# Routing of the first sequence from x centered but not scaled, first weights loaded ahead, six loads issued by ScalarE

## The reference, cut to what matters

```
x = x + 0.5 * ffn(layernorm(x))
x = x + attn(layernorm(x))
x = x + 0.5 * ffn(layernorm(x))

def layernorm(x): m, v = mean(x), var(x); return (x - m) / sqrt(v + 1e-5)
def ffn(x):       # 64 experts, 128 -> 64 -> 128, top 8
    shared = silu(x @ Ws_up) @ Ws_down
    aff = x @ centroids.T
    idx = top_k(aff + expert_biases, 8)
    w = sigmoid(aff[idx]);  w = w / (sum(w) + 1e-8)
    cw = w scattered to a 512 x 64 table
    h = silu(x @ W_up[e]);  y = h @ W_down[e]
    return shared + sum over e of y * cw[:, e]
```

## Time and profile before

| | us |
|---|---|
| median of 3 runs | 812.16 (812.0 to 812.24) |
| profiled execution | 811.96 |
| its span, first to last instruction | 809.8 |
| busy PE / DVE / ACT / POOL | 800.3 / 649.3 / 619.9 / 424.5 |

### The profile page before, as it was taken

The page is one execution under the profiler, slowest core; times in us unless marked ns, Lnnn a source line. Parts: engine busy times, 40 slices in busy tenths (PEclk is TensorE's granted clock), DMA queues, the critical chain, the costliest instruction groups (busy, mean ns, idle before and its releaser), DMA issues.

```text
span 809.8 us, 12417 instructions
## 1 busy us (share of the span) xinstructions
PE 800.3 (99%) x3686; PEld 651.4 (80%) x3686; DVE 649.3 (80%) x1410; ACT 619.9 (77%) x1189; POOL 424.5 (52%) x378
## 2 busy tenths in 40 slices
PE   8999999999999999999999999999999999999998
PEld 5778878888888888888888888888888888888786
DVE  6987979779797787967879679796887778688865
ACT  5887777778777777868787678786787777786875
POOL 3885546555455554545545355463554545454453
PEclk9999999999999999999999999999999999999999
DMA  7000000000000000000000000000000000000000
GB/s 261 29 1 14 13 1 1 0 26 2 14 1 0 26 0 13 0 0 26 0 13 0 0 26 0 13 0 0 26 0 0 0 1 27 0 1 1 14 0 14
DMA packets 15901, 11.44 MB, mean 14 GB/s; under 512 B 1664, under 2 KB 14848, under 8 KB 15872
## 3 DMA queue, kind: packets, MB, share of 16 engines
q1 hardware_dynamic: 15872, 11.08, 4.4%
HBM read 8.98 MB, written 2.10 MB: 14 GB/s over the span
## 4 chain that ended last, share of the span: by engine, by line
PE 92%; DVE 3%; ACT 2%; POOL 2%; DMA 1%; SPq 0%; issue 0%; DVEq 0%
PE up L718 14%; PE up L719 14%; PE up L720 14%; PE y_ps L718 14%; PE y_ps L720 14%; PE y_ps L719 14%; PE side L727 3%; PE side L737 2%; PE side L759 1%; PE side L758 1%; POOL g_lo L357 1%; ACT g_hi L450 1%; DVE gated L596 1%; DVE up L596 1%; DVE g_lo L605 1%; DMA wu_raw<-in_w_up 1%
## 5 line engine op out<-in xcount | busy, mean ns | idle before, releaser
L357 POOL TENSOR_TENSOR g_lo<-gated,g_hi 128x512 fp32r<-128x512 f32 x256 | 333.9, 1305 | 343.6 <-ACT g_hi L450 342.9
L442 ACT ACTIVATE up<-up 128x512 f32<-128x512 f32 x528 | 309.6, 587 | 97.5 <-PE up L720 95.3
L596 DVE TENSOR_TENSOR gated<-up,cw 128x512 f32<-128x512 f32 x256 | 175.6, 686 | 83.4 <-ACT up L442 77.2
L718 PE MATMUL y_ps<-g_hi,wd_hi 128*128 128x512 f32 x512 | 207.8, 406 | 1.0 <-POOL g_lo L357 0.9
L720 PE MATMUL y_ps<-g_hi,wd_lo 128*128 128x512 f32 x512 | 202.6, 396 | 0.0
L718 PE MATMUL up<-x_hi,wu_hi 128*128 128x512 f32 x512 | 202.2, 395 | 0.3 <-POOL wu_lo L364 0.3
L719 PE MATMUL up<-x_lo,wu_hi 128*128 128x512 f32 x512 | 202.5, 396 | 0.0
L720 PE MATMUL up<-x_hi,wu_lo 128*128 128x512 f32 x512 | 201.7, 394 | 0.0
L719 PE MATMUL y_ps<-g_lo,wd_hi 128*128 128x512 f32 x512 | 201.5, 394 | 0.0
L450 ACT CAST g_hi<-up 128x512 fp32r<-128x512 f32 x272 | 160.6, 591 | 47.6 <-DVE up L596 44.5
L596 DVE TENSOR_TENSOR up<-up,cw 128x512 f32<-128x512 f32 x256 | 176.9, 691 | 21.0 <-ACT up L442 17.2
(11 more groups left out here) (101 smaller groups left out, 487.2 us busy)
## 6 DMA issues: line engine op xcount, KB each, us to landing
x_in<-in_x SPq DMA_DIRECT2D x8, 256.0 KB, 2.8
wu_raw<-in_w_up SPq DMA_DIRECT2D x4, 512.0 KB, 6.1
wd_raw<-in_w_down SPq DMA_DIRECT2D x4, 512.0 KB, 6.9
x_res<-in_x SPq DMA_DIRECT2D x8, 256.0 KB, 2.7
out<-out_sb SPq DMA_DIRECT2D x7, 256.0 KB, 2.2
out<-out_sb SPq DMA_DIRECT2D x2, 128.0 KB, 1.8
ident<-in_ident SPq DMA_DIRECT2D x1, 64.0 KB, 2.6
sm_raw<-in_ws_up SPq DMA_DIRECT2D x2, 32.0 KB, 2.3
```

The lines of the kernel that those rows point to most:

```text
L357: nc.gpsimd.tensor_tensor(g_lo[:, i, :], gated[:, t // 2 % ORING, :], g_hi[:, i, :].bitcast(fp32), ALU.subtract).then_inc(lo_done[1], 1)
L442: nc.scalar.activation(up[i][:, :], up[i][:, :], ACT.Silu).then_inc(silu_done, 1)
L596: nc.vector.tensor_tensor(gated[:, t // 2 % ORING, :] if t % 2 else up[i][:, :], up[i][:, :], cw[ph.q][:, :], ALU.mult).then_inc(gate_done, 1)
L718: nc.tensor.matmul(o, a[0], b[0], start=start, stop=False)
```

## The change

Only the start and phase 0 are touched.

- ScalarE issues six of the small loads, before everything else on its queue. SyncE, without them, issues the first four pieces of the weights directly after x and the identity; the second x comes behind the third pair of pieces.
- x for the routing is only centered (ScalarE, with the negated mean as bias), since the order of a row's affinities and their sum with the biases need the scale only afterwards. It is transposed into `up[2]` and `up[3]`, copied to `x_raw` by VectorE, half by half, and the affinities are multiplied by rstd as the bias is added; the Tanh of the sigmoid takes half of rstd as its scale.
- x for the products is made apart: ScalarE scales the centered x into `normed[1]`, TensorE transposes it into `up[4]`, ScalarE casts that to `x_hi`, VectorE subtracts for `x_lo`, now behind `take_top`.
- GpSimd makes `wu_hi` of the first two eighths of W_up itself; ScalarE did.
- The weights are spread in halves, transposed in halves (`side0`, `side1`) and copied in halves. `late` of phase 0 is 2 for TensorE and, as `late_act`, 1 for ScalarE; both were 3.
- Fill-in products: 8, 1 and none instead of 12, 3 and 3.

```
-WARM_START, WARM_ROWS, WARM_ROUTE = 12, 3, 3
+WARM_START, WARM_ROWS = 8, 1
-    "late": 3,
+    "late": 2, "late_act": 1,
...
             load_x(0, wait=False)
-            sp.dma_start(ce_raw[:, :], cent_t).then_inc(small_in[0], 16)
             sp.dma_start(ident[:, :], ident_in).then_inc(small_in[0], 16)
-            sp.dma_start(bias_b[:, :], ebias.partition_broadcast(P)).then_inc(small_in[0], 16)
-            for h in range(2):
-                sp.dma_start(sm_raw[:, SU + h * F:SU + (h + 1) * F], ws_up).then_inc(small_in[1], 16)
-                sp.dma_start(sm_raw[h * F:(h + 1) * F, SD:SD + D], ws_down).then_inc(small_in[1], 16)
             load_pieces(0)
             load_pieces(1)
-            load_x(1)
...
             load_pieces(2)
+            load_x(1)
...
-            split_up(0)
-            split_up(1)
+            for i in range(2):
+                js = slice(i * JS, (i + 1) * JS)
+                pool.wait_ge(wu_in[0], 16)
+                nc.gpsimd.tensor_copy(wu_hi[:, js, :], wu_raw[:, js, :]).then_inc(first_hi_done, 1)
+                split_up(i)
...
-                    cw_copy(ph.q, ph.use)
+                    if ph.first:
+                        act.wait_ge(first_cw_half, 1)
+                        nc.scalar.copy(cw[0][:, half(0, T)], side0[:, half(0, T)])
+                        act.wait_ge(cw_turned[0], 1)
+                        nc.scalar.copy(cw[0][:, half(1, T)], side1[:, half(1, T)]).then_inc(cw_done[0], 1)
...
+            nc.scalar.dma_start(ce_raw[:, :], cent_t).then_inc(route_in, 16)
+            nc.scalar.dma_start(bias_b[:, :], ebias.partition_broadcast(P)).then_inc(route_in, 16)
+            for h in range(2):
+                nc.scalar.dma_start(sm_raw[:, SU + h * F:SU + (h + 1) * F], ws_up).then_inc(small_in[1], 16)
+                nc.scalar.dma_start(sm_raw[h * F:(h + 1) * F, SD:SD + D], ws_down).then_inc(small_in[1], 16)
...
+            act.wait_ge(neg_mean_done, 1)
+            for m in range(NB):
+                made = nc.scalar.activation(normed[0][:, m, :], x_in[:, m, :], ACT.Identity, bias=neg_mean[:, m:m + 1])
...
+            for m in range(NB):
+                made = nc.scalar.activation(normed[1][:, m, :], normed[0][:, m, :], ACT.Copy, scale=rstd[0][:, m:m + 1])
+            made.then_inc(first_scaled, 1)
             act.wait_ge(x_turned[0], 1)
+            nc.scalar.copy(x_hi[0][:, :], up[RING - 1][:, :]).then_inc(x_hi_done[0], 1)
+            act.wait_ge(bias_done[0], 1)
+            act.wait_ge(half_rstd_done, 1)
+            for m in range(NB):
+                made = nc.scalar.activation(sig[:, m, :], aff[:, m, :], ACT.Tanh, scale=half_rstd[:, m:m + 1])
...
+            nc.vector.tensor_scalar_mul(neg_mean[:, :], mv[0][:, :, 0], -1.0).then_inc(neg_mean_done, 1)
...
+            for m in range(NB):
+                made = nc.vector.scalar_tensor_tensor(biased[:, m, :], aff[:, m, :], rstd[0][:, m:m + 1], bias_b[:, :],
+                                                      ALU.mult, ALU.add)
+            made.then_inc(bias_done[0], 1)
             find_top(0, 0)
             take_top(0, 0)
+            dve.wait_ge(x_hi_done[0], 1)
+            nc.vector.tensor_tensor(x_lo[0][:, :], up[RING - 1][:, :], x_hi[0][:, :].bitcast(fp32), ALU.subtract).then_inc(x_lo_done[0], 1)
             select(0, 0)
...
-                        if ph.first:
-                            keep_busy(WARM_ROUTE, side0, wu_hi[:, 0, :], wu_hi[:, 0:NB, :])
                         turn_cw(ph.q, ph.use, ph.first)
```

More of the change, by code:

```diff
@@ L464, in phase @@
                 if ph.late is not None:
-                    for t in range(ph.late + 1):
+                    for t in range(ph.late_act + 1):
                         silu(ph, t)
@@ L468, in phase @@
                             high_part(ph, 0)
-                    cw_copy(ph.q, ph.use)
+                    if ph.first:
[3 more added lines that the diff above has]
+                        nc.scalar.copy(cw[0][:, half(1, T)], side1[:, half(1, T)]).then_inc(cw_done[0], 1)
+                    else:
+                        cw_copy(ph.q, ph.use)
                     if not ph.first:
@@ L472, in phase @@
                 for t in range(SLOTS):
-                    if t < NT and (ph.late is None or t > ph.late):
+                    if t < NT and (ph.late is None or t > ph.late_act):
                         silu(ph, t)
@@ L698, in _ @@
             dve.wait_ge(inv_done[0], 1)
-            nc.vector.tensor_tensor(*spread_operands, ALU.mult).then_inc(first_dup_done, 1)
+            for h in range(2):
+                nc.vector.tensor_tensor(*(o[:, half(h, NB), :, :] for o in spread_operands), ALU.mult).then_inc(first_dup_done, 1)
             split_low(wd_lo, wd_raw, wd_hi, 0, wd_hi_done, wd_lo_done[0])
@@ L768, in up_product @@
                 w = (wu_hi[:, t - 1, :], wu_lo[:, t - 1, :]) if t > 0 else small(SU, SU + P)
-                split_product(o[:, :], w, (x_hi[q][:, :], x_lo[q][:, :]), True, True).then_inc(up_done, 1)
+                if ph.first and t == 0:
+                    nc.tensor.matmul(o[:, :], w[0], x_hi[q][:, :], start=True, stop=False)
+                    nc.tensor.matmul(o[:, :], w[1], x_hi[q][:, :], start=False, stop=False)
+                    pe.wait_ge(x_lo_done[q], 1)
+                    nc.tensor.matmul(o[:, :], w[0], x_lo[q][:, :], start=False, stop=True).then_inc(up_done, 1)
+                else:
+                    split_product(o[:, :], w, (x_hi[q][:, :], x_lo[q][:, :]), True, True).then_inc(up_done, 1)
             def down_product(ph, t):
@@ L810, in phase @@
                     if t == 0:
-                        pe.wait_ge(x_lo_done[ph.q], ph.use + 1)
+                        if ph.first:
+                            pe.wait_ge(x_hi_done[0], 1)
+                        else:
+                            pe.wait_ge(x_lo_done[ph.q], ph.use + 1)
                     if t < NT and before(t - RING)[1] < NT and not (ph.first and t < RING):
@@ L861, in _ @@
                 for m in range(h * NB // 2, (h + 1) * NB // 2):
-                    last = nc.tensor.transpose(rows((side0, side1)[h], m), normed[0][:, m, :], ident[:, :])
-                last.then_inc(half_turned if h == 0 else x_turned[0], 1)
+                    last = nc.tensor.transpose(rows(up[2 + h], m), normed[0][:, m, :], ident[:, :])
+                last.then_inc(half_turned, 1)
+            pe.wait_ge(route_in, 32)
+            pe.wait_ge(half_copied, 1)
+            affinity_blocks(0, range(0, NB // 2))
+            pe.wait_ge(x_copied[0], 1)
+            affinity_blocks(0, range(NB // 2, NB)).then_inc(aff_done[0], 1)
+            pe.wait_ge(first_scaled, 1)
+            turn(up[RING - 1], lambda m: normed[1][:, m, :]).then_inc(x_turned[0], 1)
             keep_busy(WARM_ROWS, y_ps[:, :], zeros_r[:, :], g_hi[:, 0, :])
-            affinities(0, 0)
             over_phases(pe, phase)
```

59 lines of the change are left out of this document (38 added, 21 removed).

## The result

The changed kernel takes **819.31 us** (median of 4 runs, 818.87 to 819.48) against 812.17: ratio 1.0087, interval 1.0071 to 1.0103. It is 7.1 us slower; 811.6 was forecast, within 809.9 to 813.3. The profiled execution took 819.14 us.

What follows compares the result with a forecast made beforehand. TensorE's own work was taken to bound the kernel, the start only shifting it through VectorE's gating of tile 5. A routing gain of 1.1 less 0.5 for a late Silu saves 0.6 us: 812.16 becomes 811.6, range 809.9 to 813.3.

Steps and rivals of the forecast that it cites:

- The bound: Whole kernel: TensorE busy 800.3 of 809.8 us, so a change to the start only shifts its steady stream.
- sm_hi after 6.22: ScalarE's start: the load for sm_hi is there in time, sm_hi done by 6.6, sigmoid 0.25 us before VectorE wants it.
- Rival (2): ScalarE's front is late, through waiting issues or small loads landing late among the pieces (814.0); chance 0.20.
- These edits cost nothing: Start: GpSimd's casts for the first two pieces and the later second x are hidden, low parts ready at 9.4 and 11.3.
- rival (1): More comes through: late Silu 3 free (0.5), normalisations' hold avoided (0.93), 2.0 us saved, 810.1; chance 0.22.
- the 5.06: ScalarE's start: six issues end at 3.55, then table load 1.28 and first Silu 0.21, so centring can begin.
- bias add: VectorE's routing: becomes four 128x64 operations, 0.75 us taken, 0.33 more than before, bounds 0.42 and 1.68.
- the late Silu: ScalarE, phase 0: Silu 3 falls between the casts of tiles 1 and 4, delaying gating of tile 5 by 0.50 us.
- the front: Routing up to VectorE's selection: selection at 10.8 against 12.04, 1.24 ahead, taken as 1.1 us after 0.15 for slow transposes.
- my case: Main forecast for the kernel: 0.6 us saved, 811.6, spreading over 811.0 to 812.4 by its bounds; chance 0.42.
- Rival (2)'s other form: Start: ScalarE's six issues take turns with SyncE's, 5.64 us instead of 2.82, ending at 814.4.
- Rival (3): TensorE stays at or falls back to its low clock with fewer fill-ins: 813.0, or 814.5 if it lasts; chance 0.16.

Runs made afterwards that it cites:

- e1: The changed kernel with all six small loads back on SyncE, ahead of the pieces: 813.98 us.
- e15: The changed kernel with all six small loads back on SyncE ahead of the pieces and the two new tensors declared last: 812.27 us.
- e8: The changed kernel, shared-expert loads on SyncE ahead of the pieces, new tensors last, late 3 for both engines, three fill-ins behind the transposes: 811.52 us.
- e2: The changed kernel, ScalarE still issuing the six loads, but SyncE waiting for the shared expert's four before issuing the first piece: 814.17 us.
- e3: The kernel before, with only the six small loads issued by ScalarE ahead of its table load: 817.49 us.
- e9: e8 with four unused tensors behind neg_half, 128 bytes: 797.57 us.
- e4: The kernel before, with the change's two new tensors declared and never used: 813.69 us.
- e5: The changed kernel with its two new tensors, neg_mean and half_rstd, declared last: 817.00 us.
- e7: The changed kernel with the old 12, 3 and 3 fill-in products again: 819.13 us.
- e17: The changed kernel with two more unused tensors behind its own two, 128 bytes in all: 802.92 us.

## Why the prediction was wrong

**The bound was read rightly.** The start moves TensorE's stream as a whole: the 1.51 us wait at 33.40 stands, unchanged in length, at 39.12, 34.53 (e1), 33.83 (e15) and 33.42 (e8).

**The step that failed: "sm_hi after 6.22 (its last load is issued at 3.1 and a load of this kind lands after 2.1 us, so it is there)".** It was issued at 3.46 and landed after 9.1. Rival (2) named this very case, but priced it with 5.8 us and so at 814.0, and gave it part of 0.20. The 5.8 was the landing of another load, of 64 KB, between pieces in one queue. The Trainium skill ("DMA: Bandwidth & Descriptors", Queues, rings and completion order) has each DMA engine alternate between the queues that have work, a packet from each. The trace agrees as far as it goes: between 3.5 and 10 us its packet record holds, in every 0.5 us, 30 to 47 packets of SyncE's queue (mostly 4096 bytes, 159 ns each by the median) and 22 to 46 of ScalarE's (mostly 256 bytes, 18 ns). The page's packet is of 9 to 17 descriptors, and the record doesn't say whether its own packets are such groups. At about one for one, small packets wait for large ones, and the six loads go at the pieces' pace. e1, e2 and e3 show the lateness and its cure; the alternation is read from the record and not from an edit. Delay through the chain: sm_hi 6.3 late against e15 (12.61 and 6.30), selection 6.4 (17.29 and 10.85), gating of tile 1 5.3 (20.75 and 15.46), for the late spread at least escapes the hold. In time it is 5.3 (e1 against the changed kernel). The low clock behind the wait has a part in it that no run separates: x's transposes before x_hi took 1.11 in place of 0.66.

**"These edits cost nothing" leaves out a hold.** GpSimd's work on the first two pieces is itself hidden, as said, and in the changed kernel, where GpSimd had ended at 17.65 before the spread began, the spread took 0.76; 0.79 was forecast. But once the loads are punctual, VectorE's selection and spread meet the low parts. The spread took 1.74 in e2 and e15, 0.95 over the forecast, and the selection 1.40 in e8. Before, wu_lo ended at 12.49 and the spread began at 13.48. Where the hold falls depends on when the pieces come, and e2 and e15 issue them later than the change does; but the forecast's own times, low parts ready at 9.4 and 11.3 and the selection at 10.8, put it on the selection, and it is in no term. I had used such a hold in rival (1) for the normalisation and not looked for it here. The rows are regular: wherever the selection begins while GpSimd is in a low part, it ends 0.27 to 0.29 us after that part (12.77 and 12.49 before, 17.93 and 17.65 in the changed kernel, 12.72 and 12.45 in e8), and where it does not, in e1, e3 and e9, it takes 0.41 or 0.42; the spread ends 0.61 or 0.62 after (14.10 and 13.49 in e15). So even the 0.73 of the selection before had 0.3 of waiting in it. The Trainium skill ("SBUF — State Buffer", Who interferes with whom) has a VectorE instruction with two SBUF inputs contend with a GpSimd instruction that reads SBUF; the rows agree with that.

**The placement was in no step.** It is worth 1.6 (e4), 2.3 (e5) and 1.7 (e15 against e1), and the row of busy times alone would have shown it only afterwards.

**What held, and where luck helped.** In e15 the affinities end at 7.9 (7.66), the selection is at **10.85 (10.8)** with the sigmoid ready at 10.49 (10.55). But e15 has no issues on ScalarE: its centring starts at 4.94 when VectorE has negated the mean, so it is no test of the 5.06, which was the end of ScalarE's own issues, table load and first Silu. With the six issues on ScalarE the centring started at 5.37 in e2 and at 6.19 in the changed kernel, and e2, the one kernel with such issues and punctual loads, has its selection at 11.25. The bias add takes 0.86 (0.75 taken). From gating of tile 1 to tile 5 it is 4.91 us in the changed kernel and in e15, against 4.40 before and in e8: the 0.5 that the late Silu gives back. In e15 the front gains 1.19, from selection to gating of tile 1 it takes 4.61 in place of 3.50, which is 1.11 more, and the Silu costs 0.51: together +0.43, as at the next-x row, where −0.6 was forecast. One sum is off too: an issue of 0.52 (0.3) and a bias add of 1.68 (0.93 over the 0.75) end at 812.8, not at the 812.4 given as the upper bound of my case.

**Rival (2)'s other form**, ScalarE's issues taking turns with SyncE's, did not come for five of six issues: they took 0.45 to 0.59. The last took 1.29, beside one of SyncE's that took 1.22; the same issue took 0.47 in e2, where SyncE waits at that time, and 0.59 to 1.11 in e3, e5, e7 and e17. The rule of the Trainium skill that the prediction weighed ("Perfetto Trace Analysis", DMA Instruction — HWDGE) taken strictly would have doubled all six; the rows do not show that. **Rival (3)**, the low clock, was there as well. In the changed kernel's profiled execution TensorE was slow before it waited: the affinities took 1.94 us, against 1.09 in e15, and products stayed at 0.42 apart until 17.5. With eight fill-ins the affinities took 1.94 in four profiled executions (the changed kernel, e1, e9, e17) and 1.09 in four (e2, e5, e8, e15); with twelve they took 1.02 to 1.09 in all but e3's, where they stand behind a wait of 4.4 us. That points to the fewer fill-ins, as the rival said, but one execution of each kernel does not show it. Behind the late loads it made no difference: the other three executions of the changed kernel have a mean granted clock of 0.994 against 1.000 in the profiled one, as e5 with 0.993, so it had risen there and fell in the wait, and they took 818.87 to 819.48 against 819.14. Nor did twelve fill-ins help (e7); without them it cost e1's profiled execution 0.6 and e9's 0.9 over their medians. **Rival (1)** did not come; the two normalisations took 1.89 again in e15.

From 811.6: +0.7 to e15 (the hold and what else that kernel holds), +1.7 from there to e1 (placement), +5.3 to the changed kernel (late loads), in all 819.3. These are differences of medians one after another and so must add up; that the two prices stand apart is shown by e17, not by this sum.

**Open:** why x and g must both be displaced; whether the cast of sm_hi placed behind x_hi on ScalarE would alone have hidden most of the late loads (not tried); and GpSimd's low part was never moved away from the selection, so its price is read from traces and not from an edit of its own; and whether the fewer fill-ins are what leaves the clock low in some executions.

## What to carry to other kernels

A small load in a second queue is not out of the way of large ones in the first: what a consumer waits for should be issued before the large transfers, from whichever engine, and no work that doesn't need it should stand behind the wait. When work is moved forward, look at what the other engine of a shared pair does at the new time, not only whether the moved work is ready. And before a difference of 1% is put down to a change, pad the allocation: declare the new tensors in the old kernel, unused, and time that.

## What the runs showed of the hardware that was not expected

Displacing the moving tiles against the weights by 64, 128, 192 and 256 bytes gave +1.6, −14.0, −9.0 and 0 us, 1.7% at best, with TensorE's 3686 instructions unchanged. A 32 KB load went from 2.1 to 2.4 us alone to 9.1 us at the most beside 512 KB loads of another queue. A VectorE selection of 0.41 us took up to 1.40 beside GpSimd's subtraction, always ending 0.27 to 0.29 us after it. In e5 and e7 TensorE had reached its upper level (affinities in 1.09 us) and was granted 0.50 of its clock from 8.5 and 12.2 us on, in a wait of 5.38 and 5.06 us, until 18.6 and 18.9 us.
